# A three-round graph kernel, and 64 single-column copies per unit that nobody reads

## The chip, the cores and the metric

The kernel runs on one core of one Trainium2 chip. The metric is the device time of one execution in microseconds (us). The engines are TensorE (PE), VectorE (DVE), ScalarE (ACT), GpSimd (POOL) and SyncE (SP); each runs its own queue of instructions, and they meet only at semaphores.

## The reference

Inputs are 12,500 nodes with 128 features (`x`), and 200,000 edges sorted by destination (`src`, `dst`, `edge_type_4`, `edge_weight`). The function is cut here to what is computed:

```python
def _rgcn_conv(x, src, dst, edge_type, edge_weight, W, root, bias):
    xj = x[src]
    m = jnp.zeros((xj.shape[0], W.shape[2]), dtype=x.dtype)
    for r in range(W.shape[0]):                       # 4 relations
        mask = (edge_type == r).astype(x.dtype)[:, None]
        m = m + mask * (xj @ W[r])
    m = m * edge_weight[:, None]
    out = jax.ops.segment_sum(m, dst, num_segments=x.shape[0])
    return out + x @ root + bias

# layer 0: edge weights rescaled to 0..1, two rgcn convolutions with a relu between
h = jnp.maximum(_layernorm(x, axis=-1), 0.0)
x = x + L0(h)        # h = relu(_rgcn_conv(h, W1, root1, b1)); h = _rgcn_conv(h, W2, root2, b2)
# layer 1: one weighted gather and sum, then a dense product
h = jnp.maximum(_layernorm(x, axis=-1), 0.0)
x = x + L1(h)        # agg = segment_sum(edge_weight * h[src], dst); agg @ W.T + b
```

## The kernel before

There are three rounds over the edges, one for each gather and sum: two for the two convolutions, one for the last layer. The 200,000 edges are cut into 1,563 chunks of 128. Four chunks make a group (`CG`), four groups a unit (`UG`), so a unit `u` has 16 chunks and a round has 98 units; the last unit has 11 chunks. A ring of four units (`RING`) of buffers holds gathered rows.

For each chunk, GpSimd issues one indirect DMA (line 558) that gathers 128 rows of a table in HBM into `rows`. Its row numbers stand in `idx`, which VectorE writes (lines 1285 to 1292) four units ahead. Some chunks are gathered in another way: in every fourth unit one chunk goes to `spare`, row by row, by DMAs of SyncE (line 502), and in the third round in eleven units one chunk goes to `spare_a` by 128 single-row DMAs of ScalarE (line 798, `act_rows`), sixteen of them per unit, whose byte offsets are loaded from a list into registers, eight at a time (line 793). So GpSimd has 1563 - 24 - 11 = 1,528 gathers in the third round. A gather waits for its `idx`, and the second gather of every group waits until TensorE has begun the group two before (`s_begun`, `LEAD`).

In the second and third round the work of a unit is this. TensorE multiplies each gathered chunk with its `window`, a 128 x 48 one-hot matrix times the edge weights (line 1016), and sums a group in PSUM. VectorE waits for the unit (`s_agg`), writes new `idx`, adds the four sums into `acc` at columns whose number it loads from a list (line 1214 loads four of them, line 1223 adds), and in between writes the windows of unit u+4 (lines 1372 and 1376). ScalarE waits until all four sums of unit u are added (`s_acc`), copies the finished 128 nodes of tile u-1 into `tile_T` (`prep`, line 688), and then issues its single rows. TensorE multiplies `tile_T` with the last layer's weights half-way through the next unit (line 947, `finish`), VectorE adds `x_rows` and writes `st` (line 1273, `finish2`), and SyncE stores it. Nothing sets the order but each engine's own program order and the semaphores. The copies of the change read `key0`, a 128 x 1563 array of float32 in SBUF that the first round uses.

Of the kernel before, what the change touches and what calls it, by code (L numbers as in the profile page):

```python
# [4 lines left out]
P = 128  # L5
# [18 lines left out]
def build(nc, x, src, dst, etype, weight, W1, root1, b1, W2, root2, b2, W3, b3, out):  # L24
    fp32, bf16, i32 = mybir.dt.float32, mybir.dt.bfloat16, mybir.dt.int32
    ALU, ACT, AX = mybir.AluOpType, mybir.ActivationFunctionType, mybir.AxisListType.X
# [4 lines left out]
    R = W1.shape[0]  # L31
# [9 lines left out]
    NO = NU // SE  # L41
# [27 lines left out]
    with ctx:  # L69
        def sb(name, shape, dt=fp32):  # L70
            return ctx.enter_context(nc.sbuf_tensor(name, shape, dt))

        def sem(name):
            return ctx.enter_context(nc.semaphore(name))
# [5 lines left out]
        key_col, rel, key0 = sb("key_col", [P, C]), sb("rel", [P, C]), sb("key0", [P, C])  # L80
# [9 lines left out]
        single_src, single_type = sb("single_src", [NO, P], i32), sb("single_type", [NO, P], i32)  # L90
# [10 lines left out]
        lists = [win[:, a * CT * P:(a + 1) * CT * P] for a in range(4)]  # L101
# [19 lines left out]
        stats = sb("stats", [P, 2, BT, 6])  # L121
        mv = sb("mv", [P, 2, BT, 2])
        std, rstd, shift = (sb(n, [P, 2, BT]) for n in ("std", "rstd", "shift"))
        ext, extg = sb("ext", [P, 5]), sb("extg", [P, 5])
        extm, extb = sb("extm", [5, 1]), sb("extb", [5, P])
        wscale = sb("wscale", [P, 1])
# [52 lines left out]
        s_gidx, s_grow = sem("s_gidx"), sem("s_grow")  # L179
        s_gs, s_gwindow, s_gagg, s_gagg_sb, s_gmix, s_gacc = (  # L180
            sem(n) for n in ("s_gs", "s_gwindow", "s_gagg", "s_gagg_sb", "s_gmix", "s_gacc"))

        def wait(eng, s, v):

            if isinstance(v, int) and v <= 0:
                return
            eng.wait_ge(s, v)
# [6 lines left out]
        def first(b, n):  # L194

            return isinstance(b, int) and b < n

        def units(unit, first_unit=0):

            for u in range(first_unit, NU):  # L200
                unit(u // RING, u % RING)
# [43 lines left out]
        def act_number(r, u):  # L245

            return (r - 1) * (AO - 1) + u // AE - 1
# [49 lines left out]
        def stored_by(r, s, n):  # L297

            return 16 * ((0, NT // 2, NT // 2 + pairs_of(s))[r] + n)
# [318 lines left out]
        def _(eng):  # L618
# [95 lines left out]
            def finish1(t, v, n, events):  # L714

                s = v % 2
                root_of_var(t + events, s, 1)
                eng.wait_ge(s_shift, t + (events + 1))
                if not isinstance(t, int):
                    eng.wait_ge(s_stored[v // 2], n * 16 + stored_by(1, 0, 0))  # L720
                normalise(st[:, v // 2, s * 2 * D:s * 2 * D + D], fin_of(t, s)[:, 0:D], s, 0).then_inc(s_fin_a, 1)
# [55 lines left out]
            def act_rows(r, u):  # L777

                j, part = divmod(u + AE - 1, AE)
                if not 0 < j < AO:  # L780
                    return
                n = act_number(r, j * AE + 1)
                if part == 0:
                    if j == 1:
                        eng.wait_ge(s_single_at, 7)
                        for s in range(2):
                            eng.wait_ge(s_stored[s], stored_by(r, s, 0))
                    if n > 1:
                        r0, j0 = divmod(n - 2, AO - 1)
                        eng.wait_ge(s_agg, r0 * NU + (j0 + 1) * AE + 2)  # L790
                table = in_bytes[r]
                for p in range(part * P // AE, (part + 1) * P // AE, OB):
                    found = nc.values_load_multi_w_load_instructions(
                        act_at[r - 1][j:j + 1, p:p + OB], engines=(mybir.EngineType.Activation,), min_val=0,
                        max_val=table.shape[1] - row_bytes,
                        skip_runtime_bounds_check_because="the lists name nodes of the graph alone")[1]
                    for k in range(OB):
                        eng.dma_start(spare_a[p + k:p + k + 1, n % 2, :].bitcast(mybir.dt.uint8),
                                      table[0:1, bass.ds(found[k], row_bytes)]).then_inc(s_by_act[n % 2], 16)

            def fast(r):

                def unit(i, v):
                    u = i * RING + v
                    if r == 1 and not first(u, 2):
                        finish1(u - 2, (u - 2) % XR, (u - 2) // XR, NB + RAW)
                    if not first(u, 1):
                        eng.wait_ge(s_acc, u * UG + (r * NG + UG) if not isinstance(u, int) else r * NG + min(u * UG + UG, NG))
                        prep(r, u - 1, (v - 1) % 2)
                    act_rows(r, u)  # L810
                units(unit)
                prep(r, NT - 1, (NT - 1) % 2)
                if r == 1:
                    finish1_last(NB + RAW)
# [255 lines left out]
        def _(eng):  # L1070
            steps = [0]

            def link(ins):

                steps[0] += 1
                ins.then_inc(s_step, 1)
                eng.wait_ge(s_step, steps[0])
# [225 lines left out]
            def first_round():  # L1303
# [56 lines left out]
                units(unit)  # L1360
                adds(NU - 1, NU - 1, NG - (NU - 1) * UG)

            def fast(r):
                wt = sw_col if r < 2 else w_col

                def weigh(c, v, h, n, u):

                    lo, n = h * HC, min(HC, n - h * HC)
                    slots = window[:, v * UC + lo:v * UC + lo + n, :]
                    part = u * 2 + ((r - 1) * 2 * NU + h + 1)  # L1370
                    wait(eng, s_window, part - 1)
                    eng.tensor_tensor(match_ps[:, 0:n, :], iota_ps.unsqueeze(1).to_broadcast([P, n, W]),  # L1372
                                      rel[:, bass.ds(c + lo, n)].unsqueeze(2).to_broadcast([P, n, W]),
                                      ALU.is_equal).then_inc(s_eq, 1)
                    eng.wait_ge(s_eq, part)
                    eng.tensor_tensor(slots, match_ps[:, 0:n, :],  # L1376
                                      wt[:, bass.ds(c + lo, n)].unsqueeze(2).to_broadcast([P, n, W]),
                                      ALU.mult).then_inc(s_window, 1)

                if r == 1:  # L1380
                    eng.wait_ge(s_half, 2 * NU)
                    eng.wait_ge(s_own0_add, NT)
                    link(eng.tensor_copy(iota_ps, iota[:, 0:W]))
                for u in range(RING):
                    take_idx(u * UC, u, UC, r)
                for u in range(RING):
                    for h in range(2):
                        weigh(u * UC, u, h, UC, u)
                sums_ready(r)

                def unit(i, v):
                    u = i * RING + v
                    ahead = not isinstance(u, int) or u + RING < NU
                    n = chunks_of(u + RING) if ahead else 0
                    c = u * UC + RING * UC
                    if r == 2 and u > 1 and u % 2 == 0:
                        stored_out(u - 2)
                    elif r == 2 and u > 0:
                        loaded_x2(u - 1)
                    base = bases(u, len(groups_of(u)))  # L1400
                    if not first(u, 2):
                        finish(u - 2, (u - 2) % XR, (u - 2) // XR)
                    if u < NU - 1:
                        eng.wait_ge(s_agg, u + ((r - 1) * NU + 1))
                    else:
                        eng.wait_ge(s_agg_part, r)
                    if ahead:
                        take_idx(c, v, n, r)
                    for q in groups_of(u):
                        if u == NU - 1 and q == LASTQ:  # L1410
                            eng.wait_ge(s_agg, r * NU)
                        add(r, u * UG + q, base[q], agg_of(u, v, q)[:, q * W:(q + 1) * W])
                        if ahead and q % 2 == 1:
                            weigh(c, v, q // 2, n, u + RING)

                def finish(t, v, n):
                    if r == 1:
                        finish1(t, v, n, NB + RAW)
                    else:
                        finish2(t, v, n)  # L1420
                units(unit)
                if r == 1:
                    finish1_last(NB + RAW)
                else:
                    stored_out(NT - 2)
                    for t in range(NT - 2, NT):
                        finish2(t, t % XR, t // XR)
# [89 lines left out]
```

## Time and profile before

| | us |
|---|---|
| median of the two runs shown | 7904.76 |
| the two runs | 7901.24 and 7908.29 |
| span of the profiled execution, first to last instruction | 5774.9 |
| median less span: time that no row of the trace covers | 2129.9 |
| first and last gather of the third round, start in the span | 3859.43 and 5765.93 |
| GpSimd busy, share of the span | 75% |
| VectorE and ScalarE busy, share of the span | 25% and 8% |

For the profiled execution only its span is on record, not its own time by the clock of the runs. What fills the 2,130 us between the span and the median no view shows. Rows of the trace give the start of an instruction in the span, how long it took, and in brackets how long the engine had been idle before it and what ended that. Lines that begin with an engine and a q are of its sequencer: register loads, register writes and DMA issues, which do not count as busy.

### The profile page before, as it was taken

What the parts mean: (1) busy time and instruction counts of PE and PEld (TensorE: products, weight loads), DVE (VectorE), ACT (ScalarE), POOL (GpSimd) and SP (SyncE); (2) the same over time, 40 slices, a digit from 0 to 9 for tenths busy, and PEclk for the clock granted to TensorE, in tenths of its full rate; (3) what the DMA queues carried; (4) which work ended last, traced back from release to release, by engine and by line L of the source; (5) the groups of instructions that cost most, each with busy time, mean ns of one, the idle gap of its engine ahead of it and who ended that gap; (6) DMA issues with size and microseconds to landing.
All of it is one profiled execution on the core that took longest, in us unless ns stands there. A gap on an engine that the chain in (4) does not pass through costs nothing.

```text
span 5774.9 us, 61089 instructions
## 1 busy us (share of the span) xinstructions
PE 3158.5 (55%) x11399; PEld 2521.8 (44%) x11399; DVE 1415.7 (25%) x5042; ACT 439.1 (8%) x1183; POOL 4343.6 (75%) x4604
## 2 busy tenths in 40 slices
PE   3766666666666545444444444444444445444454
PEld 2655544544555434333334443434444444444443
DVE  7433333333333222122212222211111111111111
ACT  5111111111111000000000000000000000000000
POOL 7777777777777677777777777777777777777777
PEclk7878788788877655555555555555555555555555
DMA  6222222222222222222222222222222222222222
GB/s 173 82 76 74 73 75 74 73 75 74 73 75 74 61 62 62 61 60 62 62 60 61 62 62 60 62 59 60 62 62 60 62 62 60 62 62 61 60 62 58
DMA packets 285830, 392.59 MB, mean 68 GB/s; under 512 B 92011, under 2 KB 199360, under 8 KB 285440
## 3 DMA queue, kind: packets, MB, share of 16 engines
q0 software_dynamic: 147072, 301.50, 20.0%
q1 hardware_dynamic: 132736, 85.70, 4.9%
q14 instruction: 299, 2.45, 0.1%
q8 instruction: 91, 1.49, 0.1%
q10 hardware_dynamic: 5632, 1.45, 0.1%
HBM read 336.95 MB, written 51.34 MB: 67 GB/s over the span
## 4 chain that ended last, share of the span: by engine, by line
POOL 74%; issue 24%; PE 1%; DMA 1%; DVE 0%; ACT 0%; POOLq 0%; DVEq 0%
POOL rows L558 74%; DMA rows<-table,idx 1%; PE bank L975 0%; PE bank L915 0%; PE bank L893 0%; PE bank L908 0%; PE bank L923 0%; DMA table<-st 0%; DMA table<-sums 0%; DMA st<-in_src_dram 0%; PE bank L924 0%; DVE win L1342 0%; PE bank L1016 0%; DVE acc L1223 0%; POOLq L69 0%
## 5 line engine op out<-in xcount | busy, mean ns | idle before, releaser
L558 POOL DMA_INDIRECT rows<-table,idx x4532 | 4276.9, 944 | 1402.1 <-issue 1378.0
L1016 PE MATMUL bank<-win,rows 128*128 128x48 f32 x6112 | 1816.9, 424 | 1938.7 <-DMA rows<-table,idx 1917.4
L1016 PEld LDWEIGHTS bank<-win,rows 128*128 128x128 f32 x6112 | 1474.6, 317 | 2281.5 <-DMA rows<-table,idx 2261.1
L975 PE MATMUL bank<-win,rows 128*128 128x192 f32 x3080 | 850.0, 404 | 634.9 <-DMA rows<-table,idx 490.2
L975 PEld LDWEIGHTS bank<-win,rows 128*128 128x128 f32 x3080 | 587.4, 226 | 846.9 <-DMA rows<-table,idx 670.2
L1223 DVE TENSOR_TENSOR acc<-acc,bank 128x48 f32 x1173 | 237.8, 203 | 1106.0 <-PE bank L893 956.6
L1342 DVE TENSOR_SCALAR win<-iota,key,sw_col 128x192 f32<-128x192 f32 x1563 | 501.5, 391 | 18.2 <-PE bank L908 16.2
L688 ACT ACTIVATE tile_T<-acc 128x128 f32<-128x128 f32 x196 | 60.4, 309 | 2852.5 <-DVE acc L1223 2852.5
L1285 DVE TENSOR_SCALAR idx<-src_col 128x16 int32<-128x16 int32 x98 | 18.5, 191 | 829.7 <-PE bank L1016 829.7
L893 PE MATMUL bank<-sums,W1s 128*128 128x192 f32 (+1 forms) x784 | 218.7, 445 | 0.4 <-ACT sums L736 0.4
L1372 DVE TENSOR_TENSOR bank<-bank,rel 128x384 f32<-128x384 f32 x392 | 218.6, 558 | 0.7 <-issue 0.2
L1292 DVE SCALAR_TENSOR_TENSOR idx<-src_col,type_col 128x16 int32<-128x16 int32 x98 | 18.5, 191 | 772.1 <-PE bank L1016 772.1
L893 PEld LDWEIGHTS bank<-sums,W1s 128*128 128x128 f32 x784 | 205.1, 280 | 0.9 <-ACT sums L736 0.9
L1273 DVE TENSOR_TENSOR st<-bank,x_rows 128x128 f32<-128x128 f32 x98 | 28.6, 292 | 709.3 <-PE bank L947 709.3
L1094 DVE BATCH_NORM_STATS2 stats<-bank 128x6 f32<-128x128 f32 x98 | 29.2, 299 | 677.9 <-PE bank L945 677.9
L915 PE MATMUL bank<-W2s,tile_T 128*128 128x512 f32 x194 | 147.9, 858 | 0.0
L1376 DVE TENSOR_TENSOR win<-bank,w_col 128x384 f32<-128x384 f32 x196 | 109.0, 556 | 6.8
L1376 DVE TENSOR_TENSOR win<-bank,sw_col 128x384 f32<-128x384 f32 x196 | 109.0, 556 | 6.8
L623 ACT ACTIVATE std<-mv,eps 128x1 f32<-128x1 f32 (+3 forms) x127 | 37.2, 293 | 822.3 <-DVE mv L1100 822.3
L701 ACT ACTIVATE acc<-bank,b2s 128x128 f32<-128x128 f32 x98 | 36.0, 367 | 740.8 <-PE bank L924 740.8
L736 ACT ACTIVATE sums<-bank 128x384 f32<-128x384 f32 x196 | 85.6, 495 | 5.6 <-PE bank L975 5.6
L678 ACT ACTIVATE hT<-bank 128x128 f32<-128x128 f32 x98 | 27.2, 277 | 756.6 <-PE bank L901 756.6
(123 smaller groups left out, 1235.4 us busy)
## 6 DMA issues: line engine op xcount, KB each, us to landing
spare<-table SPq DMA_DIRECT2D x9088, 0.5 KB
rows<-table,idx POOLq DMA_INDIRECT x4532, 2.5
spare_a<-table ACTq DMA_DIRECT2D x2816, 0.5 KB
table<-st SPq DMA_DIRECT2D x146, 256.0 KB, 2.4
x_rows<-table SPq DMA_DIRECT2D x49, 128.0 KB
x_rows<-in_x_dram SPq DMA_DIRECT2D x48, 128.0 KB
h_rows<-table SPq DMA_DIRECT2D x48, 128.0 KB, 2.3
out_dram<-st SPq DMA_DIRECT2D x48, 128.0 KB, 2.1
```

Of the source, the lines that this page charges most:

```text
L558: eng.indirect_dma_start(out=rows[:, slot, :], out_offset=None, in_=table[:, :], in_offset=bass.IndirectOffsetOnAxis(ap=idx[:, slot:slot + ...
L623: eng.activation(std[:, p, 0:n], mv[:, p, 0:n, 1], ACT.Sqrt, bias=eps[:, 0:1]).then_inc(s_std, 1)
L688: eng.activation(tile_T[:, s, :], columns(t), ACT.Copy).then_inc(s_prep, 1)
L736: eng.activation(sums[:, v % 2, 2 * h:2 * h + w, :].rearrange("p g w -> p (g w)"), half_ps[v % 2 * 2 + h][:, 0:w * RW], ACT.Copy).then_inc ...
L893: ins = eng.matmul(mix_ps[:, 0:w], W1s[:, k, :], rhs(k), start=(k == 0), stop=(k == R - 1))
L915: eng.matmul(wide_of(t)[:, :], inner_of(t, s), W2s[:, :, :].rearrange("p r d -> p (r d)"), start=True, stop=True).then_inc(s_fin, 1)
L975: ins = eng.matmul(half_ps[v % 2 * 2 + h][:, q % 2 * RW:(q % 2 + 1) * RW], chunk_rows(0, u, q * CG + k), wide[:, v % 2, q * CG + k, :], st ...
L1016: ins = eng.matmul(agg_of(u, v, q)[:, q * W:(q + 1) * W], chunk_rows(r, u, q * CG + k), window[:, slot, :], start=(k == 0), stop=(k == n - 1))
L1223: eng.tensor_tensor(a, a, sums_ps, ALU.add).then_inc(s_acc, 1)
L1342: ins = eng.tensor_scalar(wide[:, v % 2, q * CG + k, :], iota[:, 0:RW], key0[:, bass.ds(c, 1)], sw_col[:, bass.ds(c, 1)], ALU.is_equal, AL ...
L1372: eng.tensor_tensor(match_ps[:, 0:n, :], iota_ps.unsqueeze(1).to_broadcast([P, n, W]), rel[:, bass.ds(c + lo, n)].unsqueeze(2).to_broadcas ...
L1376: eng.tensor_tensor(slots, match_ps[:, 0:n, :], wt[:, bass.ds(c + lo, n)].unsqueeze(2).to_broadcast([P, n, W]), ALU.mult).then_inc(s_windo ...
```

## The change

Two buffers of 128 x 32 float32 are added. In every unit of the third round (`r == 2`), after all that the unit did before, VectorE and ScalarE each load 2 x 16 numbers from row `u % 24` of `single_type` (a list of edge types, 0 to 3) into registers, and copy 32 columns of `key0`, one column at a time, at these numbers, into their buffer: VectorE with a multiplication by 1.0, ScalarE with the activation `Copy`. Before the copies of unit u each waits for its own last copy of unit u-1. Nobody reads the buffers.

```diff
+        side_v, side_a = sb("side_v", [P, 32]), sb("side_a", [P, 32])
+        s_side_v, s_side_a = s_gagg, s_gagg_sb
...
+            def columns_by_list(u):                      # ScalarE
+
+                j = u % NO
+                wait(eng, s_side_a, u)
+                for p in range(0, 32, 16):
+                    at = nc.values_load_multi_w_load_instructions(
+                        single_type[j:j + 1, p:p + 16], engines=(mybir.EngineType.Activation,), min_val=0, max_val=R - 1,
+                        skip_runtime_bounds_check_because="the lists name relations alone")[1]
+                    for k in range(16):
+                        ins = eng.activation(side_a[:, p + k:p + k + 1], key0[:, bass.ds(at[k], 1)], ACT.Copy)
+                ins.then_inc(s_side_a, 1)
...
                         prep(r, u - 1, (v - 1) % 2)
                     act_rows(r, u)
+                    if r == 2:
+                        columns_by_list(u)
                 units(unit)
                 prep(r, NT - 1, (NT - 1) % 2)
...
+            def columns_by_list(u):                      # VectorE: the same, but for these lines
+                wait(eng, s_side_v, u)
...
+                        ins = eng.tensor_scalar(side_v[:, p + k:p + k + 1], key0[:, bass.ds(at[k], 1)], 1.0, None, ALU.mult)
...
                         if ahead and q % 2 == 1:
                             weigh(c, v, q // 2, n, u + RING)
+                    if r == 2:
+                        columns_by_list(u)
```

VectorE's queue in the middle of the third round of the kernel after, from the second load of one unit's copies on; line 1389 is the copy with the register write (ISA) ahead of it:

```order
11305 L1385 TENSOR_LOAD single_type
11306 L1389 ISA
11307 L1389 TENSOR_SCALAR side_v<-key 128x1
11308 L1389 ISA
11309 L1389 TENSOR_SCALAR side_v<-key 128x1
11310 L1389 ISA
11311 L1389 TENSOR_SCALAR side_v<-key 128x1
```

Each copy has a register write of its own, so a unit adds 2 loads, 32 register writes and 32 copies on each engine: 66 instructions, and 98 x 66 = 6,468 on VectorE. On ScalarE it is the same number. The end of ScalarE's queue in the third round, before and then after, ahead of the jump over the general path:

```order
1641 L798 DMA spare_a<-table 1x512 x8
1642 L793 TENSOR_LOAD act_at
1643 L798 DMA spare_a<-table 1x512 x8
1644 L688 ACTIVATE tile_T<-acc 128x128 x10
1645 L839 UNCONDITIONAL_BRANCH
```

```order
8117 L813 ISA
8118 L813 ACTIVATE side_a<-key 128x1
8119 L813 ISA
8120 L813 ACTIVATE side_a<-key 128x1
8121 L691 ACTIVATE tile_T<-acc 128x128
8122 L856 UNCONDITIONAL_BRANCH
```

Before, the last ten copies of finished tiles stand in a row; now the 66 instructions of the last unit stand between the last two of them.

## Rows read from the trace of the kernel before

**Rows 1.** The page: engines, and the chain that ended last

```profile
PE 3158.5 (55%) x11399; PEld 2521.8 (44%) x11399; DVE 1415.7 (25%) x5042; ACT 439.1 (8%) x1183; POOL 4343.6 (75%) x4604
POOL 74%; issue 24%; PE 1%; DMA 1%; DVE 0%; ACT 0%; POOLq 0%; DVEq 0%
```

**Rows 2.** GpSimd's timeline where the third round begins, and its last gather

```profile
3859.43 0.94 POOL L558 DMA_INDIRECT rows<-table,idx  x1 [8.47 <-DMA table<-st]
...
5765.93 0.94 POOL L558 DMA_INDIRECT rows<-table,idx  x1 [0.30 <-issue]
```

**Rows 3.** Windows in the first and third round: us, GpSimd busy (instructions), PEclk, DMA, GB/s

```profile
700.00:1700.00 1000.00, 755.74 (x801) 0.81 0.27 74
...
4200.00:5200.00 1000.00, 755.69 (x802) 0.50 0.23 61
```

**Rows 4.** Who waited for whom from 4200 to 5774 us: total us, times, longest

```profile
ACT tile_T L688 <- DVE acc L1223: 1547.2, 81, 20.3
...
POOL rows L558 <- issue: 383.0, 1256, 0.3
```

**Rows 5.** ScalarE's timeline in one unit, then in a late one without single rows

```profile
5016.46 0.31 ACT L688 ACTIVATE tile_T<-acc 128x128 f32<-128x128 f32 x1 [19.73 <-DVE acc L1223]
5017.28 6.09 ACTq L798 DMA_DIRECT2D spare_a<-table  x16
...
5620.76 0.31 ACT L688 ACTIVATE tile_T<-acc 128x128 f32<-128x128 f32 x1 [18.36 <-DVE acc L1223]
```

**Rows 6.** Register loads: ScalarE's of eight numbers, VectorE's of four (ns min/median/max)

```profile
L793 ACTq TENSOR_LOAD <-act_at x352: 565/732/1034, 1988.3 to 5605.5; - x176
L1214 DVEq TENSOR_LOAD <-base_i x294: 337/342/751, 94.0 to 5757.0; - x147
```

**Rows 7.** ScalarE: one alone of 128 columns, seven back to back with two pointers

```profile
L688 ACT ACTIVATE tile_T<-acc 128x128 f32<-128x128 f32 x196 | 60.4, 309 | 2852.5 <-DVE acc L1223 2852.5
9.53 2.80 ACT L628 ACTIVATE acc<-acc,shift,rstd 128x128 f32<-128x128 f32 x7
L628 ACT ACTIVATE acc<-acc,shift,rstd x98: 477/477/493, 9.5 to 75.2; 128x128 f32<-128x128 f32 x97, 84x128 f32<-84x128 f32 x1
L657 ACT ACTIVATE w_col<-bank 128x512 f32<-128x512 f32 x3 | 1.5, 570 | 0.0
L657 ACT ACTIVATE w_col<-bank 128x27 f32<-128x27 f32 x1 | 0.2, 166 | 0.0
```

**Rows 8.** VectorE: one column alone, and a dependent row of four adds

```profile
L1154 DVE TENSOR_SCALAR ext<-ext x1: 153/153/153, 42.1 to 42.1; 128x1 f32<-128x1 f32 x1
1007.63 1.21 DVE L1223 TENSOR_TENSOR acc<-acc,bank 128x48 f32 x4 [8.80 <-PE bank L893]
```

**Rows 9.** VectorE's timeline over one unit of the third round

```profile
5014.27 0.17 DVE L1285 TENSOR_SCALAR idx<-src_col 128x16 int32<-128x16 int32 x1 [9.00 <-PE bank L1016]
5016.94 0.56 DVE L1376 TENSOR_TENSOR win<-bank,w_col 128x384 f32<-128x384 f32 x1
5025.10 0.29 DVE L1273 TENSOR_TENSOR st<-bank,x_rows 128x128 f32<-128x128 f32 x1 [7.61 <-PE bank L947]
5033.00 0.17 DVE L1285 TENSOR_SCALAR idx<-src_col 128x16 int32<-128x16 int32 x1 [7.60 <-PE bank L1016]
```

**Rows 10.** VectorE from SBUF to SBUF: the first round's windows (ns min/median/max)

```profile
L1342 DVE TENSOR_SCALAR win<-iota,key,sw_col x1563: 347/372/591, 74.5 to 1921.3; 128x192 f32<-128x192 f32 x196
```

**Rows 11.** The chain that ended last, its last pieces: start, us, what

```profile
5769.77 0.32 ACT tile_T L688
...
5770.14 1.24 PE bank L947 x4
...
5771.40 0.29 DVE st L1273
```

**Rows 12.** The page: its first line, and a DMA queue (packets, MB, share)

```profile
span 5774.9 us, 61089 instructions
...
q14 instruction: 299, 2.45, 0.1%
```

More of the change, by code:

```diff
@@ L1361, in first_round @@
                 adds(NU - 1, NU - 1, NG - (NU - 1) * UG)
+            def columns_by_list(u):
+                j = u % NO
+                wait(eng, s_side_v, u)
+                for p in range(0, 32, 16):
+                    at = nc.values_load_multi_w_load_instructions(
+                        single_type[j:j + 1, p:p + 16], engines=(mybir.EngineType.DVE,), min_val=0, max_val=R - 1,
+                        skip_runtime_bounds_check_because="the lists name relations alone")[1]
+                    for k in range(16):
+                        ins = eng.tensor_scalar(side_v[:, p + k:p + k + 1], key0[:, bass.ds(at[k], 1)], 1.0, None, ALU.mult)
+                ins.then_inc(s_side_v, 1)
             def fast(r):
```

## Prediction

> **What bounds the kernel now.** I read the page first. GpSimd is busy for 75% of the span, VectorE for 25% and ScalarE for 8%, and the chain of waits is 74% GpSimd and 24% "issue" [rows 1]. "Issue" is time in which GpSimd waited for nothing that the profile shows, so the chain is one queue of gathers from end to end. The timeline says at what pace: the third round's first gather starts at 3859.43 us and the last of its 1,528 at 5765.93 [rows 2], which is (5765.93 - 3859.43) / 1527 = 1.2485 us each. The windows show 801 of them in 1,000 us of the first round and 802 in the third [rows 3], although the other engines have quite different work in the first. Then I asked in the list of waits whether anything holds GpSimd up in the third round: 1,256 times it waited for "issue", 0.3 us at the longest, and for nothing else. The same list shows who is early: ScalarE waited 1547.2 of 1,574 us for VectorE's adds [rows 4].
>
> A unit of the third round has 1528 / 97.7 = 15.6 gathers, so it lasts 19.5 us; the short ones, with 15, last 18.7. What is added to VectorE or ScalarE costs nothing as long as their work of a unit stays below that, and as long as it makes nobody late on whom a gather depends.
>
> **ScalarE, part by part.** Its unit is now a `prep` of 0.31 us, then the first load, then 16 DMA issues: from 5016.46 to 5017.28 + 6.09 = 5023.37 us, or 6.9 us [rows 5]. The row says 19.73 us idle before the `prep` because issues do not count as busy; the true rest is about 12 us. In the last ten units there are no single rows, and it works 0.3 us of 18.7 [rows 5].
>
> Added are two loads of 16 numbers. A load of eight takes 0.732 us at the median, from 0.565 to 1.034 [rows 6]. VectorE's load of four takes 0.342 us, and both are near 0.09 us a number, so I take time in proportion: 1.46 us a load, 2.9 us for two, with 1.1 (no growth with the count, at the fast end) and 4.1 as ends.
>
> Added are 32 copies of one column, each with a register write. No row has such a copy. Copies out of PSUM of 512 and 27 columns take 570 and 166 ns, 0.833 ns a column; the copy of 128 columns out of SBUF takes 309 ns, so one of a single column takes about 309 - 127 x 0.833 = 203 ns alone [rows 7]. Seven activations of 477 ns back to back take 2.80 us, (2.80 - 0.477) / 6 = 0.387 us from start to start, so neighbours overlap by 0.09 us [rows 7]. That gives 0.203 - 0.09 = 0.113 us per column as the low end. The high end is 0.387, the densest row of ScalarE from SBUF that the trace has, taken over whole. I take 0.15, near the low end because these copies have neither pointer operands nor 128 columns, and a little above it for the register write. Sum: 32 x 0.15 + 2.9 = 7.7 us a unit, from 4.7 to 16.5. With 6.9 us of old work it is 14.6 us of at least 18.7. It comes after the `prep` and the single rows of its own unit, so only the `prep` of the next unit could be late for it, and that is not due for another 4 us. **Cost inside the round: nothing**, and the cover is the gathers' pace.
>
> **VectorE.** A unit's `idx` is written at 5014.27 us, the last window ends at 5016.94 + 0.56 = 5017.5, `finish2` comes at 5025.10, when TensorE lets it, and the next `idx` at 5033.00 [rows 9]. So there is a hole of 7.6 us right where the copies go, and another of 7.6 us behind `finish2`. One column takes 153 ns alone. The slowest pace of small operations that the trace shows is the dependent row of adds, 1.21 us for four of 0.20, or 0.335 us from start to start [rows 8]. I take 0.153, since back to back they can hardly be slower than alone without a dependence. Two loads at 0.342 / 4 per number cost 2.7 us [rows 6]. Sum: 32 x 0.153 + 2.7 = 7.6 us, just the hole; at the high end 32 x 0.335 + 2.7 = 13.4 us. Then `finish2` starts some 6 us late, but it ends by 5031.5, still before the next `idx` is due at 5033.00. Who waits for `finish2` is TensorE, one unit on, for the PSUM tile, and the store. What GpSimd needs, `idx`, is four units ahead. **Cost: nothing.**
>
> **The waits.** Each engine waits for its own last copy of the unit before. That was 10 us earlier, and costs nothing.
>
> **The end.** Here the cover is gone, because after the last gather nothing paces the others. Before: `prep` for the last two tiles runs at 5769.77, TensorE follows at 5770.14 and VectorE's last `finish2` is at 5771.40 [rows 11]. Now, as the order of ScalarE's queue shows, its last unit does `prep` 96, then its 32 copies, and only then `prep` 97. VectorE's copies of the last unit stand ahead of both last `finish2`, beside ScalarE's and no longer than they. So the end moves by ScalarE's 7.7 us, from 4.7 to 16.5. There is one such place; at the start of the round everything added is behind the first gathers.
>
> **Sum.** Span 5774.9 + 7.7 = 5782.6 us. The median is 2129.9 us above the span, and no view covers that. I carry it over unchanged: 7904.76 + 7.7 = **7912.5 us**, 0.1% slower, far below the 2% or so that a measurement of this kernel can tell from no change.
>
> **Where a page speaks against this.** Line 1342 in the first round is a VectorE operation in float32 that reads and writes SBUF, 1,563 times [rows 10]. It fills 0.37 us x 16 = 6 us of each unit, more than the 4.9 us of copies that the change adds, and GpSimd still makes 801 gathers per 1,000 us there against 802 [rows 3]. The Trainium skill, "SBUF — State Buffer", section "Who interferes with whom", says that such one-source operations can take a port pair that VectorE shares with GpSimd, that the other engine is then fully blocked, and that descriptors of GpSimd's DMAs are not written meanwhile. By that rule the copies would slow the gathers; by the rows the sum stays as it is.
>
> **Rivals.**
> *A blocked GpSimd.* Every VectorE copy stops the descriptor work of a gather for its whole length: 98 x 32 x 0.153 = 480 us, which gives 8393 us with the end; this is the outcome of the page just named. For it: single columns, with ports taken and given back 32 times per unit, have no row. Against it: 801 against 802. It reaches 2% from 158 / 3136 = 0.05 us lost per copy. 5%.
> *ScalarE as the bound.* If a column costs the high 0.387 us and a load 2 us, its unit is 6.9 + 16.5 = 23.4 us against 19.5. `prep` is then late, TensorE's `finish` in the middle of its queue waits, groups begin late, and GpSimd stops at `s_begun`. The 88 units with single rows lose 3.9 us each, 343 us, and with the end 16.5: 8264 us, slower. It decides from (19.5 - 6.9 - 2.9) / 32 = 0.30 us per column; 0.35 would give 2%. For it: the register write per column is untested. Against it: 0.30 is twice what I work out, and a copy alone takes 0.203. 6%, of which a third within 2%.
> *The part outside the span grows.* 2129.9 us over 61,089 instructions [rows 12] is 35 ns each; if it is spent per instruction, 12,936 more add 451 us: 8363 us. For it: nothing shows what that time is. Against it: 2.45 MB of instructions come through one queue within the span at 0.1% of the DMA engines [rows 12], so they are fetched while the program runs. 4%.
> *It does not do what it says* (the copies are not there or cost no time): 7904.8 us, no change. 2%.
> *Faster.* Nothing is removed from GpSimd's queue and nothing comes earlier. 1% for what I do not see.
>
> **How the numbers follow.** The forecast, 7912.5, has 82%. Its own range is 4.7 to 16.5 us above the median, widened by 20 us to each side because two runs, 7 us apart, are few to place a median: 7889 to 7941. The fourth rival lies in it. I extend the top to 7965 for a ScalarE that is only just the bound, and leave the other rivals out: 7889 to 7965. Faster by over 2%: 1%. Slower by over 2%: 5 + 4 + 4 = 13%. Within: 86%.
>
> **What would show it.** In the changed kernel's windows of the third round GpSimd still makes 802 gathers per 1,000 us, with no wait but "issue"; ScalarE's copies stand 0.11 to 0.2 us apart and its loads take 1.4 us; `finish2` starts at about the same place in the unit; between the last two `prep` there are some 8 us. The prediction is wrong if gathers take over 1.25 us from start to start while VectorE copies (a blocked GpSimd), if GpSimd or TensorE waits for `tile_T` (ScalarE as the bound), or if the span stays and the time grows.

## The result: 101 us slower, outside the range, and not on the chain that the profile of before showed

| | median, us | runs |
|---|---|---|
| before | 7904.76 | 7901.24 and 7908.29 |
| changed | 8005.66 | 8001.48 and 8009.85 |

The ratio is 1.0118, with an interval from 1.0076 to 1.0161. The forecast was 7912.5, in a range from 7889 to 7965. "Within 2%" came true, by luck as the rest will show; "+7.7 us" did not. One finding of the later runs is needed to read these numbers: the same kernel takes 5,777 us on some chips and 7,782 to 7,934 us on others, steadily on each, and the profile of before was of the first kind while the two times above are of the second.

The page of the changed kernel is of the second kind too. Its span is not 5,775 us but 8007.9, two microseconds short of its run of 8009.85. First its engines, its queue of instructions and its chain that ended last (compare [rows 1, 12]):

```profile
span 8007.9 us, 74025 instructions
...
PE 2982.5 (37%) x11399; PEld 2498.4 (31%) x11399; DVE 1800.1 (22%) x8178; ACT 838.1 (10%) x4319; POOL 4351.4 (54%) x4604
...
q14 instruction: 401, 3.28, 0.1%
...
SPq 58%; issue 37%; another core or an unknown queue 1%; DVE 1%; ACT 1%; PE 0%; POOL 0%; DMA 0%; DVEq 0%; ACTq 0%
SPq L505 47%; SPq L500 9%; SPq L391 0%; SPq L431 0%; POOL rows L561 0%; SPq L454 0%; DVE stats L1111 0%; ACT acc L631 0%; SPq L448 0%; SPq L474 0%; DVE win L1359 0%; PE bank L992 0%; ACT rows L631 0%; DVE mv L1117 0%
```

GpSimd is 0% of the chain. What ends last, all the way back, is the queue of SyncE: the issues of single rows (line 505, line 502 in the kernel before) and the register loads for them (line 500). GpSimd is busy as long as before in microseconds (4351 against 4344) and waits in between. Windows of 1,000 us in the first and third round answer to [rows 3]; the columns are busy time (count) of PE, PEld, DVE, ACT and POOL, then granted clock, DMA share and GB/s:

```profile
700.00:1700.00 1000.00, 502.51 (x1950) 405.25 (x1951) 250.92 (x865) 93.42 (x238) 593.18 (x627) 0.71 0.21 58
6000.00:7000.00 1000.00, 312.66 (x1227) 277.75 (x1226) 262.63 (x1529) 157.62 (x1213) 534.86 (x566) 0.50 0.17 43
```

627 and 566 gathers where [rows 3] has 801 and 802, and already in the first round, which the change does not touch. So, to judge by the changed kernel, all but 2 us of the 2,130 between the old span and the median were not outside the span; the queues were slower throughout. How they are slower is in the view of line 505, ns min/median/max, with the same line of the changed kernel on a quiet chip (run e4, below) in the fence behind it:

```profile
L505 SPq MOVE spare<-table x9088: 1/29/1412, 175.8 to 7960.4; - x198
L505 SPq DMA_DIRECT2D spare<-table x9088: 1/228/1430, 175.9 to 7960.5; - x198
```

```profile
L505 SPq MOVE spare<-table x9088: 29/29/29, 97.2 to 5677.7; - x198
L505 SPq DMA_DIRECT2D spare<-table x9088: 227/228/341, 97.3 to 5677.7; - x198
```

A register write takes 29 ns every time on the quiet chip. Here the median is the same, but some take 700 or 1,400 ns. In the records, they come in stretches in which one instruction after the other starts some 0.7 us behind the last, or twice that. I call such a queue held. Counting pairs of neighbouring records that start 0.64 to 0.78 or 1.35 to 1.48 us apart, SyncE has 4,835 in 19,777 records here and 62 on the quiet chip; 4,556 in the kernel before on a holding chip (run e12).

### The profile page after: what moved, and what is told of

It reads as the page before. It is cut to its first block, busy times and chain, and to the rows that moved or that the text cites. A ratio compares the mean times of both kernels' runs of the same rounds, so it can differ in the third digit from the quotient of the medians.

```text
span 8007.9 us, 74025 instructions
## 1 busy us (share of the span) xinstructions
PE 2982.5 (37%) x11399; PEld 2498.4 (31%) x11399; DVE 1800.1 (22%) x8178; ACT 838.1 (10%) x4319; POOL 4351.4 (54%) x4604
## 4 chain that ended last, share of the span: by engine, by line
SPq 58%; issue 37%; another core or an unknown queue 1%; DVE 1%; ACT 1%; PE 0%; POOL 0%; DMA 0%; DVEq 0%; ACTq 0%
SPq L505 47%; SPq L500 9%; SPq L391 0%; SPq L431 0%; POOL rows L561 0%; SPq L454 0%; DVE stats L1111 0%; ACT acc L631 0%; SPq L448 0%; SPq L474 0%; DVE win L1359 0%; PE bank L992 0%; ACT rows L631 0%; DVE mv L1117 0%
## 5 line engine op out<-in xcount | busy, mean ns | idle before, releaser
L1033 PE MATMUL bank<-win,rows 128*128 128x48 f32 x6112 | 1642.1, 418 | 1508.5 <-DMA rows<-table,idx 1347.2
L992 PE MATMUL bank<-win,rows 128*128 128x192 f32 x3080 | 797.8, 404 | 740.8 <-issue 261.6
L813 ACT ACTIVATE side_a<-key 128x1 f32 x3136 | 397.2, 194 | 1732.7 <-issue 1730.5
L1389 DVE TENSOR_SCALAR side_v<-key 128x1 f32 x3136 | 400.9, 154 | 716.0 <-issue 714.3
L1033 PE MATMUL bank<-win,spare 128*128 128x48 f32 x96 | 31.8, 431 | 1085.9 <-DMA spare<-table 1085.9
L1033 PEld LDWEIGHTS bank<-win,spare 128*128 128x128 f32 x96 | 24.0, 311 | 1093.6 <-DMA spare<-table 1093.6
L964 PE MATMUL bank<-W3T,tile_T 128*128 128x128 f32 x196 | 77.0, 497 | 757.3 <-ACT tile_T L691 638.9
L910 PEld LDWEIGHTS bank<-sums,W1s 128*128 128x128 f32 x784 | 187.4, 266 | 330.0 <-ACT sums L739 218.3
L964 PEld LDWEIGHTS bank<-W3T,tile_T 128*128 128x128 f32 x196 | 50.3, 317 | 769.0 <-ACT tile_T L691 648.2
L1123 DVE RECIPROCAL rstd<-std 128x1 f32<-128x1 f32 (+3 forms) x127 | 21.0, 166 | 808.9 <-ACT std L626 555.5
```

Of the source, the lines that this page charges most:

```text
L813: ins = eng.activation(side_a[:, p + k:p + k + 1], key0[:, bass.ds(at[k], 1)], ACT.Copy)
L910: ins = eng.matmul(mix_ps[:, 0:w], W1s[:, k, :], rhs(k), start=(k == 0), stop=(k == R - 1))
L964: eng.matmul(fin_of(t, s)[:, 0:D], tile_T[:, s, :], W3T[:, :], start=True, stop=True).then_inc(s_fin, 1)
L992: ins = eng.matmul(half_ps[v % 2 * 2 + h][:, q % 2 * RW:(q % 2 + 1) * RW], chunk_rows(0, u, q * CG + k), wide[:, v % 2, q * CG + k, :], st ...
L1033: ins = eng.matmul(agg_of(u, v, q)[:, q * W:(q + 1) * W], chunk_rows(r, u, q * CG + k), window[:, slot, :], start=(k == 0), stop=(k == n - 1))
L1389: ins = eng.tensor_scalar(side_v[:, p + k:p + k + 1], key0[:, bass.ds(at[k], 1)], 1.0, None, ALU.mult)
```

## Experiments

The expectations quoted below give their explanations letters. The main one is "theory Q" from the start; its content changed twice, and each expectation says how it stood. The kernel before was timed beside every group of runs. It took 5776.56 us (chip 6, the first four runs), 5776.62 (chip 13, the next four), 7918.56 (chip 14, the replays e8 to e11), 7800.87 and 7793.59 (chip 2, the last six). "Quiet" stands below for the first two, "holding" for the others.

### The kernel before, once more, and one engine at a time, on a quiet chip

e0 is the kernel before with no edit.

> The kernel before, unchanged, to have a trace whose span covers its time. Theory Q (held queues: in timed executions the register writes and DMA issues of SyncE, ScalarE and VectorE are at times held for 0.7 us each, and SyncE's and ScalarE's single rows, not GpSimd's pace, set the time): time about 7905 us, span within some 10 us of it, SyncE's register writes (29 ns in the first trace) held for about 700 ns in some tenth of the cases in all three rounds, GpSimd at about 560 to 630 gathers per 1,000 us instead of 802. Theory O (what the prediction assumed: 2,130 us lie outside the span): span 5775 us again and 802 gathers per 1,000 us.

Measured: 5775.95 us, ratio 0.9999 [0.9990, 1.0009]. The span is 5773.6 us beside a run of 5775.42, so nothing but 2 us lies around it. Theory O is refuted in its first half (no 2,130 us outside), and theory Q's "in timed executions" is wrong too: this execution was timed, and held nothing. It is the chip.

e1 drops the call on ScalarE, e2 the one on VectorE:

```diff
                     act_rows(r, u)
-                    if r == 2:                  # e1
-                        columns_by_list(u)
...
                             weigh(c, v, q // 2, n, u + RING)
-                    if r == 2:                  # e2
-                        columns_by_list(u)
```

> The copies on VectorE alone; ScalarE's are left out (nobody reads either). Theory Q: VectorE is early for what others need, so 0 to +30 us against before. Rival G (VectorE's copies block GpSimd's gathers): most of the +101 us, and gathers over 1.25 us apart while VectorE copies.

> The copies on ScalarE alone; VectorE's are left out. Theory Q: ScalarE's held queue makes its copies of finished tiles and its single rows late, so most of the +101 us, +60 to +110. Rival G: 0.

Measured: 5781.49 us each, ratio 1.0008 [0.9999, 1.0018], for both. GpSimd makes 801 gathers per 1,000 us of the third round in both. Neither 101 us nor rival G is seen on this chip.

e3 keeps both engines' copies but takes loads and register writes out:

```diff
-                    at = nc.values_load_multi_w_load_instructions(
-                        single_type[j:j + 1, p:p + 16], ...)[1]
-                        ins = eng.activation(side_a[:, p + k:p + k + 1], key0[:, bass.ds(at[k], 1)], ACT.Copy)
+                        ins = eng.activation(side_a[:, p + k:p + k + 1], key0[:, k % R:k % R + 1], ACT.Copy)
-                        ins = eng.tensor_scalar(side_v[:, p + k:p + k + 1], key0[:, bass.ds(at[k], 1)], 1.0, None, ALU.mult)
+                        ins = eng.tensor_scalar(side_v[:, p + k:p + k + 1], key0[:, k % R:k % R + 1], 1.0, None, ALU.mult)
```

> Both engines copy 32 columns a unit, but at column numbers 0 to 3 written in the program: no loads and no register writes, half of the added instructions. Theory Q: what costs are instructions of the queue that can be held, above all loads and register writes, so under a third of +101 us: 0 to +35. Rival W (the copies themselves cost, as work on the engines): +70 to +101.

Measured: 5779.46 us, ratio 1.0004 [0.9995, 1.0014], +2.9: the 32 copies at the end alone, 3.08 us in ScalarE's timeline there.

### The changed kernel on a quiet chip

> The changed kernel, unchanged, beside the kernel before on one chip. The four runs above gave 5776.6 us for the kernel before, not 7904.8, with a span of the same length, and no held queue. Theory Q now reads: where no queue is held, the change costs what it adds behind the last gather, here about 5.6 us (32 copies at 0.098 and two loads of 1.1 to 1.3 us on ScalarE), so 5782 us; where queues are held, as in the trace of the changed kernel, it costs about 100 us of 7,900. Rival L: the two engines together cost more than either alone (5.0 us each), up to 100 us, on any chip.

Measured: 5782.33 us against 5776.62, ratio 1.0009 [1.0000, 1.0019], **+5.7 us**. Rival L is refuted. The end of ScalarE's timeline of this run, which answers to [rows 11]:

```profile
5769.50 0.31 ACT L691 ACTIVATE tile_T<-acc 128x128 f32<-128x128 f32 x1 [7.26 <-DVE acc L1240]
5770.64 1.67 ACT L813 ACTIVATE side_a<-key 128x1 f32 x16 [0.83 <-issue]
5773.25 0.69 ACT L813 ACTIVATE side_a<-key 128x1 f32 x6 [0.95 <-issue]
5774.11 1.08 ACT L813 ACTIVATE side_a<-key 128x1 f32 x10 [0.17 <-issue]
5775.10 0.29 ACT L691 ACTIVATE tile_T<-acc 128x128 f32<-128x128 f32 x1
```

Between the last two `prep` there are 5775.10 - 5769.50 = 5.6 us, and that is the whole cost. Sixteen copies span 1.67 us, so they start (1.67 - 0.19) / 15 = 0.099 us apart. The views of the lines of the loads and copies, ns min/median/max:

```profile
L809 ACTq TENSOR_LOAD <-single_type x196: 1019/1102/1409, 3855.8 to 5772.1; - x196
L813 ACTq FUSED_REGOPS  x3136: 37/37/37, 3857.0 to 5774.9; - x196
L813 ACT ACTIVATE side_a<-key x3136: 188/191/203, 3857.1 to 5775.0; 128x1 f32 x196
...
L1385 DVEq TENSOR_LOAD <-single_type x196: 1095/1115/1134, 3884.3 to 5772.3; - x196
L1389 DVE TENSOR_SCALAR side_v<-key x3136: 153/154/156, 3885.5 to 5775.7; 128x1 f32 x196
```

And its windows and waits of the third round:

```profile
4200.00:5200.00 1000.00, 755.75 (x802) 0.50 0.23 62
```

```profile
POOL rows L561 <- issue: 382.7, 1255, 0.3
```

GpSimd still makes 802 gathers and waits for nothing but "issue", with 3,136 copies of VectorE beside it.

### When ScalarE does become the bound

```diff
                     if r == 2:
+                        wait(eng, s_side_a, u)
+                        for b in range(2):
+                            columns_again(u, b)     # 32 more each, into side_b, with two loads each
                         columns_by_list(u)
```

> The changed kernel with 96 instead of 32 columns and 6 instead of 2 loads per unit on ScalarE. Theory Q and the prediction's rival B agree on the mechanism: ScalarE's unit becomes 6.9 + 3 x 5.6 = 23.7 us against 19.5, so it is the bound, 88 units lose some 4.2 us: +370 us, and +17 at the end, about 6160 us; TensorE waits for tile_T and for spare_a, GpSimd for TensorE. If ScalarE's lateness is absorbed elsewhere: only the end, about 5794 us.

Measured on chip 13: 6126.07 us, ratio 1.0605 [1.0588, 1.0623], +349 us where +387 was expected. The waits of the third round:

```profile
PEld bank L977 <- ACT tile_T L691: 809.3, 78, 11.5
DVE st L1303 <- PE bank L977: 797.4, 83, 11.6
PE bank L977 <- ACT tile_T L691: 796.7, 78, 11.3
```

`prep` comes every 23.4 us instead of 19.9 as in e4 (median from start to start in the third round; 23.7 was worked out). TensorE waits for `tile_T` 78 times, and the time goes up. So the forecast's rival of a bound ScalarE works as described, at the size described; the change just does not reach it.

### Longer queues, not held ones

```diff
+                        for _ in range(7):
+                            eng.sem_inc((s_gs, s_gmix, s_gacc)[r])       # SyncE, ahead of each single row
...
+                        for _ in range(7):
+                            eng.sem_inc((s_gidx, s_grow)[r - 1])         # ScalarE, ahead of each single row
```

> The kernel before with seven increments of an unused semaphore ahead of each single-row DMA of SyncE and of ScalarE, to make these queues the bound on a chip that does not hold them. At 50 ns each SyncE's unit grows from 13.5 to about 25 us, so about 7500 us; if an increment takes 20 ns only, 18 us a unit and little change.

> The same with the copies of the change on both engines. If a longer queue of SyncE alone hides ScalarE's copies, the difference to the run before is under 20 us. If the queues that are held cost because ScalarE's and SyncE's lateness add up, +60 to +200 us.

Measured on chip 13: 8392.23 and 8393.88 us, a difference of **1.7 us**. The 7,500 us expected for e6 was too low by 890. The chain of both pages is SyncE's, as on a holding chip (e6 first, then e7):

```profile
SPq 54%; issue 43%; POOL 1%; DVE 1%; PE 1%; ACT 1%; DMA 0%; POOLq 0%; DVEq 0%; ACTq 0%
```

```profile
SPq 54%; issue 44%; POOL 1%; DVE 1%; ACT 1%; PE 0%; DMA 0%; ACTq 0%; POOLq 0%; DVEq 0%
```

With SyncE's queue as the bound and nothing held, both engines' copies are free, and even the end is hidden. That the bound is another queue does not explain the 101 us; the holding is needed. e6 also has 80,000 more instructions than before, and SyncE held 60 times in 82,257 records: a dense queue does not bring the holding about on this chip.

### Replaying the held time

From the trace of 8,008 us and that of e4 I worked out how late each single row, load and copy was, and put that time into the kernels as increments of unused semaphores (a list `HELD` of counts, one per DMA or copy; `for _ in range(next(HELD['SP'])): eng.sem_inc(...)`).

> The kernel before, with the held time of the 8,008 us trace written in: ahead of each single-row DMA of SyncE and ScalarE stand as many increments of an unused semaphore (59 ns each on SyncE, 73 on ScalarE, as measured) as that instruction was late there against the same kernel on a chip that holds nothing: 3,609 us in all on SyncE, 1,234 on ScalarE. If that alone makes the slow times: about 7,900 us. Theory Q: 80 to 130 us less than the replay of the changed kernel. Rival S (the copies cost there because SyncE's queue was held more): under 20 us less, since both replays hold SyncE equally.

> The changed kernel with the same increments, and with those of the copies as well (635 us of held time on ScalarE's copies and their register writes and loads, 437 on VectorE's). If held queues are the whole difference between 5782 and 8006 us: 7950 to 8050 us. Under 7500: something else was slow there too.

> The replay of the changed kernel without VectorE's copies. Theory Q: ScalarE's copies make its copies of finished tiles and its single rows late, so within 20 us of the replay of the changed kernel. Rival V (VectorE's idx or finish2 are late there): 50 us or more below it.

> The replay of the changed kernel, but its copies are not held: they take 5.6 us a unit as on a quiet chip, while the single rows are held as before. Theory Q1 (the copies cost because they were held themselves): near the replay of the kernel before. Theory Q2 (their own 5.6 us is enough, since the single rows' held time has used up ScalarE's slack): half of the difference or more stays.

Measured, on a holding chip: 12875.06, 12923.90, 12900.00 and 12905.45 us. The held time came on top of the real one, so the test of "about 7,900" was not made. The differences (+49 for both engines, +25 without VectorE's copies, +30 with copies that were not lengthened) are of kernels in which ScalarE is much longer than in the real one, and tell the theories apart only so far: VectorE's copies are worth 24 us there, short of rival V's 50 and above theory Q's 20, and with copies that were not lengthened 30 of the 49 us stay, which is Q2's "half or more". One thing they do show: SyncE's queue has four times the records (80,567 for 19,777) and is held about as often, 5,164 times against 4,556 in e12. So its own instructions do not bring it about one by one; what the two have alike is told at the end of the missing pairs.

> The replay of the held time in the kernel before. On a chip that holds nothing: about 7,900 us if held instructions of SyncE and ScalarE are the whole of the slow times. On one that holds queues it is held twice and gives 12,875 us again.

> The replay of the changed kernel. On a chip that holds nothing: 7,950 to 8,050 us, and 50 to 130 us over the replay of the kernel before. On one that holds queues 12,924 us again.

Measured on chip 2, also a holding one: 12780.05 and 12831.32, +51. Whether the replay gives 7,900 us on a quiet chip is not known.

### The missing pairs, on one holding chip

> The kernel before once more. On a chip that holds queues (7,905 us): a trace with SyncE held in about 4,800 instructions, like the changed kernel's, and a third round some 100 us shorter; TensorE waits for tile_T in fewer than half of the 634 us of the changed kernel. On one that holds nothing: 5776 us, as before.

> The copies on ScalarE alone. On a chip that holds queues, theory Q: +60 to +100 us against before, since TensorE waits for ScalarE's tile_T; rival V (VectorE's copies are as much to blame, by late finish2, idx or windows): about half, +50. On a chip that holds nothing: +5 us, as before.

> Both engines copy 32 columns a unit at numbers written in the program: no loads, no register writes. Theory Q is out by the last two traces (SyncE waits for nobody in the third round there, yet its queue is held 136 us longer with ScalarE's copies). Theory S: SyncE's queue is the bound where queues are held, and it is held more when another queue works through loads and register writes. Then on a chip that holds queues: 0 to +30 us, and SyncE's held time in the third round as in the second. Rival S2 (any instruction of another engine does it): +80 to +150. On a chip that holds nothing: +3, as before.

> The copies on VectorE alone, with loads and register writes. Theory S on a chip that holds queues: +50 to +150 us, like ScalarE's alone (+148), since it is not ScalarE's lateness that costs. If only ScalarE shares what holds SyncE (both issue single rows): 0 to +20. On a chip that holds nothing: +5, as before.

| chip 2 | added instructions | median, us | of before | ratio |
|---|---|---|---|---|
| e12: before | 0 | 7801.42 | 7800.87 | 0.9997 [0.9984, 1.0011] |
| e13: ScalarE alone | 6,468 | 7948.70 | 7800.87 | 1.0189 [1.0163, 1.0215] |
| e17: VectorE alone | 6,468 | 7905.01 | 7793.59 | 1.0154 [1.0130, 1.0177] |
| e16: both, fixed columns | 6,272 | 7904.85 | 7793.59 | 1.0144 [1.0122, 1.0165] |

Two expectations were missed on the way: TensorE waits 380 us for `tile_T` in e12, more than half of 634, and ScalarE alone costs 148 us, above the 100 of theory Q. VectorE alone costs 111 us, where theory Q in its first form allowed 30. Copies with no load and no register write cost the same 111, where theory S allowed 30. That leaves S2: any instructions of another engine do it, as far as VectorE's and ScalarE's were tried.

The waits of the third round show how tempting theory Q was. First the kernel before (e12), then ScalarE alone (e13):

```profile
PE bank L1016 <- DMA spare<-table: 523.9, 25, 31.2
...
PE bank L947 <- ACT tile_T L688: 380.3, 24, 17.9
```

```profile
PE bank L964 <- ACT tile_T L691: 550.7, 41, 21.3
...
PE bank L1033 <- DMA spare<-table: 349.4, 24, 25.3
```

TensorE waits 170 us longer for ScalarE's `tile_T`, which would make up the 148. But it waits 174 us less for SyncE's row, so the sum is the same; something late was only exchanged for something else late. Who is the bound is told by who never waits. SyncE's own waits in e12 and e13, from 5200 us to the end, the longest two:

```profile
SPq L444 <- DVE st L1238: 32.6, 1, 32.6
SPq L471 <- DVE st L1273: 31.5, 2, 29.0
```

```profile
SPq L447 <- DVE st L1255: 32.7, 1, 32.7
SPq L480 <- DVE st L1290: 10.2, 2, 5.3
```

One is at the end of the second round and the rest at the end of the third; in between SyncE waits for nobody. The chain of waits from 5,600 to 7,700 us says the same in both, by line (e12, then e13):

```profile
by line: SPq L502 50.0%; issue 38.6%; SPq L497 9.9%; SPq L451 0.8%; SPq L471 0.7%
```

```profile
by line: SPq L505 50.3%; issue 38.6%; SPq L500 9.7%; SPq L474 0.8%; SPq L454 0.7%
```

It is all SyncE and its gaps. So I added up SyncE's queue: for every two neighbouring records that both belong to single rows (load, register write or issue; 6,482 pairs in a round), the time from start to start. "Held" is that sum less the same pairs at the medians of e0. A round runs from its first gather to the next round's, the third to the end.

| us | second round | its queue | third round | its queue | of it held |
|---|---|---|---|---|---|
| e0, quiet | 1916 | 1351 | 1915 | 1334 | 40 |
| e12, before | 2718 | 2637 | 2555 | 2459 | 1166 |
| e13, ScalarE alone | 2720 | 2611 | 2707 | 2596 | 1302 |
| e17, VectorE alone | 2714 | 2622 | 2668 | 2559 | 1265 |
| e16, both, fixed | 2731 | 2646 | 2658 | 2559 | 1265 |
| the changed kernel | 2754 | 2662 | 2690 | 2579 | 1285 |

The second round is the same to 17 us in the four kernels of chip 2. The third is 152, 113 and 103 us longer than in e12, and SyncE's queue is 136, 100 and 100 us longer. The count of pairs is the same, and none of them contains a wait for a semaphore, so by this reckoning the whole of that is held time. The same 3,072 row issues are held longer while other engines have more to do. SyncE does not wait for them; it is slower beside them.

The traces show one thing more: when the queues are held. Call gathers that start at most 1.3 us apart a run of gathers, and sort all pairs of neighbouring records of SyncE by how many gathers of such a run have started before them. The table gives the share of pairs that are held (by the two ranges of the first section) in the third round, and in two last rows over the whole of two other traces:

| share held | over 1.3 us after the last gather | 1st to 2nd | 3rd to 4th | 5th to 8th | 9th and later |
|---|---|---|---|---|---|
| e12, before | 9% | 4% | 17% | 41% | 87% |
| e13, ScalarE alone | 8% | 8% | 30% | 69% | 90% |
| e17, VectorE alone | 8% | 10% | 35% | 59% | 84% |
| e16, both, fixed | 8% | 11% | 34% | 65% | 90% |
| the changed kernel | 9% | 13% | 38% | 78% | 96% |
| e8, before, replay, whole | 1% | 8% | 24% | 43% | 79% |
| e0, quiet, whole | 3% of 31 | 2% | 0% | 0% | 0.3% |

On a holding chip SyncE is held where GpSimd has been gathering without a break, and nearly always from the ninth gather on. In e8, 64,378 of SyncE's pairs stand where no gather runs, and 588 of them are held; of the 16,188 beside gathers 4,576 are. That fits four times the records held about as often: the kernel has the same 4,596 gathers. With the added instructions the holding sets in earlier in a run, in the third round; in the second, where nothing is added, the share beside the 3rd and 4th gather is 23% to 29% in the four kernels of chip 2. There is also a sign of how the queues share it: in e12, within one run of gathers, starts are at 6523.16 (ScalarE), 6523.86 (SyncE), 6524.56 and 6524.57 (both), 6525.26 (ScalarE), 6525.96 (SyncE) and 6526.66 us (ScalarE), as if the held queues together had little more than one start every 0.7 us. Then any added instruction could cost SyncE a turn; but that is a reading of a few records, not a test. Gathers alone do not hold anything either: in e0 they run almost without a break.

## Why the prediction was wrong, step by step

**The step that failed** is "Cost inside the round: nothing", for ScalarE, and "Cost: nothing", for VectorE. On the chips that were timed that term is about 100 us: 101 in the measurement, and 148, 111 and 111 in e13, e17 and e16, of which 136, 100 and 100 us are found inside the third round as held time of SyncE's queue. It was put at nothing because "the cover is the gathers' pace", and that rests on the sum's "The median is 2129.9 us above the span, and no view covers that", carried over unchanged. A span of 5,775 and a time of 7,905 could not belong to one execution; e0, e12 and the page of the changed kernel show spans 2 us short of their runs. With it fell the first claim, that "the chain is one queue of gathers from end to end". That holds on quiet chips. On the ones timed SyncE's held queue is the chain, and a cover of gathers at 1.2485 us did not exist there: in a unit of 27 us GpSimd, VectorE and ScalarE all had more slack than I counted, and the cost came by a way that needs none of it. That the ratio is within 2% all the same is luck: 148 us in e13 is 1.9%.

**The rivals.** The nearest was "The part outside the span grows", with 35 ns for each added instruction. It was the right suspicion in the wrong place: the time does grow with added instructions, by 101 us for 12,936 (8 ns each) in the measurement, and by 17 to 23 ns each on chip 2, inside the span, as held time of SyncE. Its "against", that instructions are fetched within the span, was beside the point. "A blocked GpSimd" is refuted where it can be seen: 802 gathers with 3,136 VectorE copies in e4 [rows 3]. On a holding chip the gathers of the changed kernel take 0.946 us at the mean for 0.945 before. With it goes the outcome by the Trainium skill, "SBUF — State Buffer", section "Who interferes with whom", which ties the blocking to conditions on the operands; copies of one column of float32 from SBUF to SBUF did not slow the gathers, and the trace decides. "ScalarE as the bound" was not what happened, and was priced well: e5 gives its mechanism and 23.4 us a unit for the 23.7 expected.

**The parts that held**, on a chip like the one of the profile. ScalarE's copies start 0.099 us apart (0.113 as the low end, 0.15 taken); a load of sixteen takes 1.10 us (1.46 taken, since time goes less than in proportion to the count: eight take 0.73); the sum is 5.4 instead of 7.7 us. VectorE's copy takes 154 ns (153). `finish2` comes 10.5 us behind the unit's `idx` (5024.50 against 5013.96 in e4's timeline) and came 10.8 behind it before [rows 9]. The end moved by ScalarE's copies and no more: +5.7 us for +7.7, within the 4.7 to 16.5 given. On the timed chips this part cannot be told from the rest.

**What stays open.** What holds the queues, and why on some chips only, no view shows. It goes with runs of gathers, as the last table shows, but other things run beside them (TensorE above all), and no run takes the gathers away or spaces them out on a holding chip. Whether the recording of the trace has a part in it is not known either: every run has its span recorded. That it is not brought about by the queue's own count of instructions is seen in e6 and e8; that it grows with what VectorE and ScalarE execute is seen in e13, e16 and e17, and that they share turns with SyncE is only suggested. The two engines together cost 101 us on the chip first measured, and 148 and 111 alone on chip 2. The pair with both engines' listed copies was not run on chip 2, so whether the costs add up or saturate is not known. That the first measurement's 101 us is the same thing rests on the changed kernel's trace, whose third round has the same held share, and not on a trace of the kernel before from that chip.

## What to carry to other kernels

Before anything is argued from a profile, lay its span beside the time that is to be predicted: if they differ by more than a few microseconds, it is the profile of another situation, and the bound that it shows need not be the bound of the timed runs. Where two engines' waits change places, ask which queue waits for nobody, and add up that queue from start to start. Cover on the chain of one chip is no cover against a cost that comes through the speed of a queue that the change does not touch.

## What was not expected of the hardware

- One kernel, four chips: 5776.6 us on two, 7,794 to 7,801 and 7918.6 us on two others, with records of SyncE and ScalarE held for 0.7 us at a time in one and not in the other. Held are the single-row DMA issues, the register writes and loads between them, and with the change also VectorE's and ScalarE's copies; GpSimd's gathers still take 0.946 us at the mean.
- Added instructions on VectorE or ScalarE, of which nobody waits for a result, made SyncE's queue 100 to 136 us longer in a round on a holding chip.
- On a holding chip SyncE's queue is held beside unbroken gathers: 87% of its pairs from the ninth gather on and 4% beside the first two (e12, third round); in e8 1% where no gather runs.
- An increment of a semaphore costs 59 ns from start to start in SyncE's queue and 72 in ScalarE's on a quiet chip (e6), with 17 ns as its own record. A register load of sixteen numbers takes 1.10 us (e4, ScalarE), of eight 0.73 [rows 6], of four 0.34 [rows 6].
